# Attention and spiking feed-forward layer on one core: transfers joined to 40 a unit, the shift row sent by way of DRAM, differences loaded in four pieces, the shift's vector steps spread

## The chip, the cores and the metric

The kernel runs on one core of a Trainium2 chip, as one program. The metric is the device time of that program in microseconds (us). The engines are TensorE (PE), VectorE (DVE), ScalarE (ACT), GpSimd (POOL) and SyncE (SP); SP only issues DMA transfers here.

## The reference

One layer on x of shape (2, 2048, 256), all in float32:

```python
xn = layernorm(x)                                # per token
q, k, v = split(xn @ w_qkv)                      # 16 heads of 16
q, k = irfft(rfft(q) * sigmoid(mask)), irfft(rfft(k) * sigmoid(mask))
attn = softmax(q @ k.T / 4) @ v                  # per batch and head, 2048 x 2048 scores
a = attn @ w_out + b_out
y = square(relu(xn @ W_fc.T)) @ W_proj.T         # 256 -> 1024 -> 256
# five steps: mem = 0.9 * mem + y - (mem > 1); spikes += (mem > 1)
out = x + a + spikes / 5
```

## The kernel before

**Stages.** A first stage of about 110 us normalises x block by block, projects queries and keys (the spectral filter is folded into their weights), splits each into a high and a low part, and stores both to the DRAM tensor `qk_scratch`; values stay in SBUF. Then come 32 units, one for each head and batch (unit i = 2h + b), and a short last stage projects the attention's output and adds everything.

**A unit.** The scores of a unit are 2048 keys by 2048 queries. They are made transposed, 128 keys by 512 queries at a time, so a unit has 64 steps m (`MINI`): 4 query quarters of 16 key tiles. PE works through them in quads of 4 steps, 16 quads a unit. In each quad it does four things: scores for ACT's exponentials (`next_score`, L806); scores of a later unit's queries against keys for the row maxima (`maximum`, L773), 16 steps (`LEAD`) ahead of use; a share of the feed-forward layer (L826, L831); and, last in the quad, the four probabilities tiles of the quad before times the values (`times_v`, L821, 32 matmuls). The first quad of a quarter is an opening quad (`opening_quad`).

**Maxima and shift.** DVE reduces each maximum tile to `pmax` (L1032), one a step. When half of a unit's queries have their maxima, `split_shift` makes the shift row in four links: the negated maximum `nmax` (L1051), its high part (L1055), its low part (L1058), and a 32x32 transpose to `shiftT` (L1066). SP moves `shiftT` to `shift_rows` (`store_shift`, L361), and `first_score` (L792) adds that row to the scores through a matmul with ones. A half's row is needed at steps 0 and 32. PE's maxima go through three PSUM banks (`PLACES`), so `maximum` n+3 waits until DVE has reduced maximum n.

**Differences.** Only the first three key tiles of a quarter are computed from the keys. Every later tile accumulates on a bank that still holds the scores of the tile three before it, so it needs the key difference `delta`: POOL subtracts keys staged in `tail` (`load_stage` L335, `subtract_keys` L483), the result goes to `delta_scratch` (`store_delta`, L342), and SP loads it to `delta_sb` (`load_delta`, L351) in the pieces `PIECES`. Difference columns 0 to 127 serve step 3 of a quarter, 128 to 639 serve steps 4 to 7. Piece 0 of the next unit may be loaded only when the last quarter of this unit is done with those columns, and is needed at step 3 of the next unit.

**Who issues what.** All transfers of the units stand in SP's one queue, in the order of `head(h, b)`, and SP issues them one after the other, waiting in place:

```python
                for piece in range(len(PIECES)):
                    sp.wait_ge(exp_done, MINI * i + MINI - TB + (piece + 2) * QUAD)
                    load_delta(i + 1, piece)
```

A unit issues 76 transfers: 8 of keys, 8 of queries, 16 of staged keys, 8 that store differences, 12 that load them, 16 of shift, 8 of outputs (`move_output`, L371). POOL meanwhile squares the feed-forward's hidden values (L507) and runs the spiking steps (L522 to L541) from about step 47 on, one instruction behind the other.

## Time and profile before

| | |
|---|---|
| median of 3 runs | 1758.84 us (1754.17 to 1760.1) |
| the profiled execution, its own time | 1755.41 us |
| its span, first to last instruction | 1753.6 us |
| mean granted TensorE clock | 0.977 of 2.4 GHz |
| busy: PE, DVE, ACT, POOL | 93%, 86%, 67%, 45% of the span |
| DMA packets | 150776, 156.83 MB |

The profile is of one execution. PE is a matmul on TensorE and PEld the load of its weights, which runs beside matmuls. "A <- B" in a wait means that A stood idle until B was done. SPq is SP's queue: the time in which it issues a transfer. A row of the chain of waits names what the end of the program depended on at that time.

### The profile page before, as it was taken

Reading aid. Unit: us, or ns where it says so; the run is one execution under the profiler, and the core shown is the slowest. Engines: PE = TensorE matmul, PEld = TensorE weight load, DVE = VectorE, ACT = ScalarE, POOL = GpSimd, SP = SyncE. Lnnn points to the kernel's source line nnn. Section 1 sums busy time; section 2 is a strip of 40 time slices with the busy share of each in tenths; the row PEclk is TensorE's granted clock in tenths of the full one; section 3 lists DMA queues with packets and bytes.
Section 4 is the critical chain, followed back from the end, with each engine's and each line's share of the span. In section 5 each row is a group of like instructions: output and inputs, shape, how many; then the busy total and the mean of one; then the engine's idle time right before and its main releaser. Section 6 shows DMA issues by size and latency. Waiting matters only on the chain.

```text
span 1753.6 us, 60281 instructions
## 1 busy us (share of the span) xinstructions
PE 1634.4 (93%) x24366; PEld 1220.9 (70%) x24366; DVE 1506.6 (86%) x2782; ACT 1177.1 (67%) x2274; POOL 787.4 (45%) x1075
## 2 busy tenths in 40 slices
PE   9998999999999999999899999999999999999898
PEld 6566677677677677777676776776766776767677
DVE  7887898888898889889898898988988888889784
ACT  5546677677676677667676676776776676777572
POOL 2103345555444455555444455554344555544344
PEclk9999999999999999999999999999999999999999
DMA  6761233233222332333222323332223233322423
GB/s 225 231 224 47 69 87 82 66 87 83 80 67 71 84 80 71 83 85 82 68 74 75 84 65 84 85 84 73 68 76 85 70 78 86 83 69 73 134 58 100
DMA packets 150776, 156.83 MB, mean 89 GB/s; under 512 B 74464, under 2 KB 113248, under 8 KB 150496
## 3 DMA queue, kind: packets, MB, share of 16 engines
q1 hardware_dynamic: 147040, 149.75, 31.1%
q8 instruction: 192, 3.15, 0.7%
q10 hardware_dynamic: 3456, 3.21, 0.6%
q14 instruction: 88, 0.72, 0.1%
HBM read 119.80 MB, written 27.79 MB: 84 GB/s over the span
## 4 chain that ended last, share of the span: by engine, by line
PE 62%; DVE 16%; SPq 13%; DMA 4%; issue 3%; ACT 2%; ACTq 0%; POOL 0%; DVEq 0%; POOLq 0%
PE banks L821 22%; PE ring L773 14%; DVE pmax L1032 11%; PE ring L806 10%; PE banks L831 6%; SPq L361 4%; DMA delta_sb<-delta_scratch 4%; PE banks L826 3%; SPq L351 3%; DVE shift L1055 2%; SPq L371 2%; SPq L335 2%; ACT probs L626 2%; PE ring L942 2%; SPq L317 1%
## 5 line engine op out<-in xcount | busy, mean ns | idle before, releaser
L626 ACT ACTIVATE probs<-ring 128x512 f32<-128x512 f32 x2048 | 1076.0, 601 | 485.2 <-PE ring L806 303.7
L1032 DVE TENSOR_REDUCE pmax<-ring 128x1 f32<-128x512 f32 x2000 | 1246.5, 681 | 106.6 <-PE ring L773 98.1
L773 PE MATMUL ring<-kst,qst 64*128 64x512 f32 x2000 | 812.6, 451 | 42.3 <-DVE pmax L1032 42.3
L806 PE MATMUL ring<-qst,delta_sb 64*128 64x512 f32 x1664 | 607.9, 454 | 58.0 <-DMA delta_sb<-delta_scratch 56.4
L821 PE MATMUL banks<-probs,vst 128*32 128x128 f32 x16384 | 564.8, 279 | 0.0
L821 PEld LDWEIGHTS banks<-probs,vst 128*32 128x32 f32 x16384 | 424.1, 111 | 141.9 <-ACT probs L626 99.2
L773 PEld LDWEIGHTS ring<-kst,qst 64*128 64x128 f32 x2000 | 376.8, 188 | 180.2 <-issue 99.8
L806 PEld LDWEIGHTS ring<-qst,delta_sb 64*128 64x128 f32 x1664 | 283.1, 189 | 122.1 <-DMA delta_sb<-delta_scratch 69.8
L826 PE MATMUL banks<-xnT,wfc_sb 64*128 64x128 f32 x2016 | 279.5, 281 | 1.5 <-ACT relu_sb L631 1.5
L826 PEld LDWEIGHTS banks<-xnT,wfc_sb 64*128 64x128 f32 x2016 | 275.2, 197 | 4.9 <-ACT relu_sb L631 1.9
L831 PE MATMUL banks<-wproj_sb,hid_sb 64*128 64x256 f32 x1024 | 263.3, 377 | 0.0
L831 PEld LDWEIGHTS banks<-wproj_sb,hid_sb 64*128 64x128 f32 x1024 | 189.7, 187 | 14.2 <-ACT relu_sb L631 0.2
L792 PE MATMUL ring<-qst,kst 64*128 64x512 f32 x384 | 156.0, 470 | 10.0 <-DMA shift_rows<-shiftT 10.0
L522 POOL TENSOR_TENSOR lif<-lif 128x256 f32<-128x256 f32 x32 | 19.6, 612 | 247.3 <-ACT y_sb L646 247.3
L507 POOL TENSOR_TENSOR hid_sb<-relu_sb 128x512 f32<-128x512 f32 x64 | 66.5, 1039 | 141.7 <-ACT relu_sb L631 141.7
L794 PE MATMUL ring<-shift_rows,ones 64*128 64x512 f32 x384 | 128.0, 394 | 0.0
L483 POOL TENSOR_TENSOR tail<-tail 128x416 f32<-128x416 f32 x32 | 34.5, 1079 | 200.8 <-DMA tail<-qk_scratch 200.8
L489 POOL TENSOR_TENSOR tail<-tail 128x208 f32<-128x208 f32 x32 | 20.2, 630 | 230.8 <-ACT tail L593 230.8
L532 POOL TENSOR_SCALAR lif<-lif 128x256 f32<-128x256 f32 x128 | 109.1, 852 | 10.8
L533 POOL TENSOR_SCALAR lif<-lif 128x256 f32<-128x256 f32 x128 | 109.3, 854 | 8.0
L1100 DVE STREAM_TRANSPOSE o_sb<-banks 128x256 f32<-128x256 f32 x64 | 28.8, 450 | 93.5 <-PE banks L821 92.6
L529 POOL TENSOR_TENSOR lif<-lif 128x256 f32<-128x256 f32 x128 | 94.1, 735 | 10.0
(97 smaller groups left out, 1113.4 us busy)
## 6 DMA issues: line engine op xcount, KB each, us to landing
kst<-qk_scratch SPq DMA_DIRECT2D x256, 128.0 KB, 2.7
qst<-qk_scratch SPq DMA_DIRECT2D x256, 128.0 KB, 2.9
delta_sb<-delta_scratch SPq DMA_DIRECT2D x256, 64.0 KB, 1.9
tail<-qk_scratch SPq DMA_DIRECT2D x512, 26.0 KB, 2.2
delta_sb<-delta_scratch SPq DMA_DIRECT2D x128, 80.0 KB, 2.1
qk_scratch<-attnT SPq DMA_DIRECT2D x32, 256.0 KB, 3.0
shift_rows<-shiftT SPq DMA_DIRECT2D x512, 2.0 KB
delta_scratch<-tail SPq DMA_DIRECT2D x256, 26.0 KB, 2.0
```

Of the source, the lines that this page charges most:

```text
L529: pool.tensor_tensor(mem, upd, spks[(step + 1) % 2], ALU.subtract).then_inc(lif_step, 1)
L532: pool.tensor_scalar(spks[step % 2], mem, 1.0, None, ALU.is_gt)
L533: pool.tensor_scalar(decayed, mem, BETA, None, ALU.mult).then_inc(lif_step, 1)
L626: act.activation(probs[:, g % PS, :], score_bank(g), ACT.Exp, scale=SCALE).then_inc(exp_done, 1)
L773: pe.matmul(max_bank(x), qst[b][rows, tile * P:(tile + 1) * P], kst[b][rows, chunk * BLK:(chunk + 1) * BLK], start=True, stop=True).then_i ...
L792: pe.matmul(score_bank(g), kst[b][rows, kt * P:(kt + 1) * P], qst[b][rows, q:q + BLK], start=True, stop=False)
L794: pe.matmul(score_bank(g), ones[rows, :], shift_rows[rows, q:q + BLK], start=False, stop=True).then_inc(score_ready, 1)
L806: pe.matmul(score_bank(g), delta_sb[rows, at:at + P], qst[b][rows, q:q + BLK], start=False, stop=True, skip_group_check=True).then_inc(sco ...
L821: mm = pe.matmul(po[32 * j:32 * (j + 1), quarter * P:(quarter + 1) * P], vst[u % 2][:, kt, :], quarters[:, j], start=(kt == 0), stop=(kt = ...
L826: return pe.matmul(misc[:, (f % 4) * P:(f % 4 + 1) * P], wfc_sb[rows_of(side), c, f * P:(f + 1) * P], xnT[rows_of(side), c, tile * P:(tile ...
L831: return pe.matmul(misc[:, 0:D], hid_sb[rows_of(side), f, :], wproj_sb[rows_of(side), f, :], start=start, stop=(f == FC - 1 and side == 0))
L1032: dve.tensor_reduce(pmax[:, tile, chunk:chunk + 1], max_bank(x), AX, ALU.max).then_inc(mx_taken, 1)
```

## The change

Keys, queries, staged keys, differences and the shift row are transferred by fewer and larger DMAs, 40 a unit; the rows of a key (and of a query) lie interleaved in their 64 partitions instead of in groups of 32. The shift row goes from `shiftT` to a new DRAM tensor `shift_scratch` in one transfer and from there to `shift_rows` in two, with a wait on SP between them. The differences have a fourth piece: columns 0 to 127 alone, loaded 4 steps earlier in the last quarter and ahead of `move_output(i, 0)`; the columns from 128 on follow it. In the first half of a unit the staged keys now stand first in SP's queue, and the queries ahead of the shift. On DVE the four links stand after four successive maxima (steps 16 to 19 of a half, before all four after step 15), and the high part is made by adding a column of zeros (`shift[:, 16:24]`) instead of by a cast. On POOL `subtract_keys` stands ahead of `square`.

```diff
-PIECES = ((0, 5 * P), (5 * P, 9 * P), (9 * P, 13 * P))
+PIECES = ((0, P), (P, 5 * P), (5 * P, 9 * P), (9 * P, 13 * P))
...
 USES = 3
-KEYS = 4 * 16
+KEYS = 2 * 16
 QUERIES = 4 * 16
-SHIFT = 8 * 16
-STAGED = 16 * 16
-STORED = 8 * 16
-PIECE = 4 * 16
...
-                keys = qk_dram[1, h, :, :, tok].rearrange("d r t -> (d r) t")
-                for group in range(4):
-                    sp.dma_start(kst[b][group * 2 * DH:(group + 1) * 2 * DH, cols].bitcast(F32),
+                keys = qk_dram[1, h, :, :, tok].rearrange("d r (g t) -> (d r) g t", g=1).broadcast_to([2 * DH, 2, HALF])
+                for side in range(2):
+                    sp.dma_start(kst[b][side * SIDE:(side + 1) * SIDE, cols].bitcast(F32),
                                  keys).then_inc(keys_in[b][piece], 16)
...
                     for part in range(2):
-                        r = side * SIDE + part * 2 * DH
                         queries = qk_dram[0, h, :, part:part + 1, tok].broadcast_to([DH, 2, HALF])
-                        sp.dma_start(qst[b][r:r + 2 * DH, cols].bitcast(F32), queries).then_inc(queries_in[b][piece], 16)
+                        sp.dma_start(qst[b][side * SIDE + part:(side + 1) * SIDE:2, cols].bitcast(F32),
+                                     queries).then_inc(queries_in[b][piece], 16)
...
                 h, b = divmod(u, B)
-                for seg in range(SEGS):
-                    for k in range(2):
-                        at = b * S + k * HOP + seg * SEG
-                        sp.dma_start(stage[seg * DH:(seg + 1) * DH, k, :, :],
-                                     qk_dram[1, h, :, :, at:at + SEG]).then_inc(staged, 16)
+                for k in range(2):
+                    at = b * S + k * HOP
+                    for r in range(2):
+                        src = qk_dram[1, h, :, r, at:at + DELTA].rearrange("d (g x) -> d g x", x=SEG)
+                        sp.dma_start(stage[:, k, r, :], src).then_inc(staged, 16)
...
                 sp.wait_ge(delta_low, u + 1)
-                for seg in range(SEGS):
-                    sp.dma_start(delta_dram[u % 2, :, :, seg * SEG:(seg + 1) * SEG],
-                                 delta_pair[seg * DH:(seg + 1) * DH]).then_inc(delta_stored, 16)
+                for r in range(2):
+                    dst = delta_dram[u % 2, :, r, :].rearrange("d (g x) -> d g x", x=SEG)
+                    sp.dma_start(dst, delta_pair[:, r, :]).then_inc(delta_stored, 16)
...
-                cols = slice(*PIECES[piece])
-                src = delta_dram[u % 2, :, :, cols].rearrange("d r t -> (d r) t")
+                lo, hi = PIECES[piece]
+                src = delta_dram[u % 2, :, :, lo:hi].rearrange("d r (g t) -> (d r) g t", g=1)
                 sp.wait_ge(delta_stored, STORED * (u + 1))
-                for group in range(4):
-                    sp.dma_start(delta_sb[group * 2 * DH:(group + 1) * 2 * DH, cols].bitcast(F32),
-                                 src).then_inc(delta_in[piece], 16)
-
-            def store_shift(n, half):
+                for side in range(2):
+                    sp.dma_start(delta_sb[side * SIDE:(side + 1) * SIDE, lo:hi].bitcast(F32),
+                                 src.broadcast_to([2 * DH, 2, hi - lo])).then_inc(delta_in[piece], 16)
+
+            def store_shift(n):
                 sp.wait_ge(shift_turned, n + 1)
-                cols = slice(half * HALF, (half + 1) * HALF)
+                sp.dma_start(shift_dram[n % 2].rearrange("c (j q) -> j c q", j=4), shiftT[:, :]).then_inc(shift_stored, 16)
+
+            def load_shift(n, half):
+
+                sp.wait_ge(shift_stored, 16 * (n + 1))
+                src = shift_dram[n % 2, 0:TB, :].rearrange("(r t) x -> r (t x)", r=2)
                 for side in range(2):
-                    dst = shift_rows[side * SIDE:side * SIDE + 2, cols].rearrange("r (t j q) -> r t j q", j=4, q=32)
-                    for j in range(4):
-                        sp.dma_start(dst[:, :, j, :].bitcast(F32), shiftT[32 * j:32 * j + 16, :]).then_inc(shift_in, 16)
+                    dst = shift_rows[side * SIDE:side * SIDE + 2, half * HALF:(half + 1) * HALF]
+                    sp.dma_start(dst.bitcast(F32), src).then_inc(shift_in, 16)
...
             def head(h, b, last=False):
                 i = 2 * h + b
                 sp.wait_ge(exp_done, MINI * i + QUAD)
+                if not last:
+                    load_stage(i + 1)
                 if i and not last:
                     load_keys(h + b, 1 - b, 1)
-                if not last:
-                    load_stage(i + 1)
-                store_shift(2 * i + 1, 1)
+                    load_queries(h + b, 1 - b, 1)
+                store_shift(2 * i + 1)
+                load_shift(2 * i + 1, 1)
                 if i:
                     move_output(i - 1, 1)
-                if i and not last:
-                    load_queries(h + b, 1 - b, 1)
+                sp.wait_ge(exp_done, MINI * i + MINI // 2 + QUAD)
                 if h < H - 1:
-                    sp.wait_ge(exp_done, MINI * i + MINI // 2 + QUAD)
                     load_queries(h + 1, b, 0)
                 if last:
                     sp.wait_ge(misc_full, use(i - 1, UP_B) + 1)
                     store_delta(i + 1)
-                    store_shift(2 * i + 2, 0)
+                    store_shift(2 * i + 2)
+                    load_shift(2 * i + 2, 0)
                 if h < H - 1:
                     sp.wait_ge(exp_done, MINI * i + MINI - TB + QUAD)
                     load_keys(h + 1, b, 0)
-                move_output(i, 0)
-                if not last:
-                    for piece in range(len(PIECES)):
-                        sp.wait_ge(exp_done, MINI * i + MINI - TB + (piece + 2) * QUAD)
-                        load_delta(i + 1, piece)
+                for piece in range(0 if last else len(PIECES)):
+                    sp.wait_ge(exp_done, MINI * i + MINI - TB + (piece + 1) * QUAD)
+                    load_delta(i + 1, piece)
+                    if piece == 0:
+                        move_output(i, 0)
+                if last:
+                    move_output(i, 0)
             for i in range(2 * (H - 1)):
                 head(i // 2, i % 2)
...
                     stage_v(h + b, 1 - b, MINI * i + PS)
+                if not last:
+                    subtract_keys(i + 1)
                 square(i, 1, UP_B)
                 if not last:
-                    subtract_keys(i + 1)
                     low_delta(i + 1)
                 n = LIF_LINKS * i
...
                                       negate=True).then_inc(max_step, 1)
                 if link == 1:
                     dve.wait_ge(max_step, 2 * n + 1)
-                    dve.tensor_copy(shift[:, 0:8].bitcast(F32R), nmax[:]).then_inc(max_step, 1)
+                    if n == 0:
+                        dve.wait_ge(shift_blank, 1)
+                    dve.tensor_tensor(shift[:, 0:8].bitcast(F32R), nmax[:], shift[:, 16:24], ALU.add).then_inc(max_step, 1)
                 if link == 2:
...
                     scale_output(2 * i - 1)
-                if m == LEAD - 1:
-                    for link in range(4):
-                        split_shift(link, 2 * i + 1, 1, CHUNKS * (i + 1))
+                if 0 <= m - LEAD < 4:
+                    split_shift(m - LEAD, 2 * i + 1, 1, CHUNKS * (i + 1))
```

Two places in the order of the instructions, each as the program issues them. The first is **DVE** around the shift row that is made in the second half of a unit; the names are those of the section on the kernel. Before:

```order
L1032 TENSOR_REDUCE pmax<-ring 128x1 [waits mx_ready] x4
L1051 TENSOR_REDUCE nmax<-pmax 128x8 [waits mx_taken]
L1055 CAST shift<-nmax 128x8 [waits max_step]
L1058 TENSOR_TENSOR shift<-nmax,shift 128x8 [waits max_step]
L1066 STREAM_TRANSPOSE shiftT<-shift 128x32 [waits shift_in,shift_split]
L1032 TENSOR_REDUCE pmax<-ring 128x1 [waits mx_ready] x8
L1120 STREAM_TRANSPOSE o_turned<-o_scaled 128x256 [waits out_moved1_0,normalised]
```

After the change:

```order
L1043 TENSOR_REDUCE pmax<-ring 128x1 [waits mx_ready] x5
L1062 TENSOR_REDUCE nmax<-pmax 128x8 [waits mx_taken]
L1043 TENSOR_REDUCE pmax<-ring 128x1 [waits mx_ready]
L1068 TENSOR_TENSOR shift<-nmax,shift 128x8 [waits max_step]
L1043 TENSOR_REDUCE pmax<-ring 128x1 [waits mx_ready]
L1071 TENSOR_TENSOR shift<-nmax,shift 128x8 [waits max_step]
L1043 TENSOR_REDUCE pmax<-ring 128x1 [waits mx_ready]
L1077 STREAM_TRANSPOSE shiftT<-shift 128x32 [waits shift_in,shift_split]
L1043 TENSOR_REDUCE pmax<-ring 128x1 [waits mx_ready] x4
L1131 STREAM_TRANSPOSE o_turned<-o_scaled 128x256 [waits out_moved1_0,normalised]
```

The links no longer follow each other: one maximum stands between any two of them, and the transpose comes four maxima later. The second place is **SP** at the end of a unit, from the stored differences to the first loads of the next unit's differences. Before:

```order
L342 DMA delta_scratch<-tail 32x1x208 [waits delta_low]
L342 DMA delta_scratch<-tail 32x1x208 x7
L361 DMA shift_rows<-shiftT 2x8x32 [waits shift_turned]
L361 DMA shift_rows<-shiftT 2x8x32 x7
L317 DMA kst<-qk_scratch 32x1024 [waits exp_done]
L317 DMA kst<-qk_scratch 32x1024 x3
L371 DMA attnT<-o_turned 16x8x32 [waits out_turned]
L371 DMA attnT<-o_turned 16x8x32 x3
L351 DMA delta_sb<-delta_scratch 32x640 [waits delta_stored,exp_done]
L351 DMA delta_sb<-delta_scratch 32x640 x3
```

After the change:

```order
L345 DMA delta_scratch<-tail 16x8x208 [waits delta_low]
L345 DMA delta_scratch<-tail 16x8x208
L359 DMA shift_scratch<-shiftT 4x32x32 [waits shift_turned]
L367 DMA shift_rows<-shift_scratch 2x1024 [waits shift_stored]
L367 DMA shift_rows<-shift_scratch 2x1024
L319 DMA kst<-qk_scratch 64x1x1024 [waits exp_done]
L319 DMA kst<-qk_scratch 64x1x1024
L353 DMA delta_sb<-delta_scratch 64x1x128 [waits delta_stored,exp_done]
L353 DMA delta_sb<-delta_scratch 64x1x128
L377 DMA attnT<-o_turned 16x8x32 [waits out_turned]
L377 DMA attnT<-o_turned 16x8x32 x3
L353 DMA delta_sb<-delta_scratch 64x1x512 [waits delta_stored,exp_done]
L353 DMA delta_sb<-delta_scratch 64x1x512
```

Between `shift_turned` and the first load of differences there were 16 issues and there are now 5, with a wait for `shift_stored` among them; the four issues of outputs stand now between the first and the second piece.

## Rows read from the trace of the kernel before

**Rows 1.** The page: busy time of an engine; engines' shares of the chain that ended last.

```profile
PE 1634.4 (93%) x24366; PEld 1220.9 (70%) x24366; DVE 1506.6 (86%) x2782; ACT 1177.1 (67%) x2274; POOL 787.4 (45%) x1075
...
PE 62%; DVE 16%; SPq 13%; DMA 4%; issue 3%; ACT 2%; ACTq 0%; POOL 0%; DVEq 0%; POOLq 0%
```

**Rows 2.** Who waited for whom: us in total, times, longest wait in us.

```profile
PEld ring L806 <- DMA delta_sb<-delta_scratch: 69.8, 31, 3.4
PEld ring L773 <- DVE pmax L1032: 62.1, 69, 1.4
...
PEld ring L792 <- DMA shift_rows<-shiftT: 12.0, 7, 5.8
```

**Rows 3.** The chain in order of time, 376 to 430 us: start us, us, what.

```profile
376.85 1.18 PE banks L821 x32
...
380.88 1.06 PE banks L821 x32
...
390.66 1.01 PE banks L821 x32
...
398.82 1.01 PE banks L821 x32
...
401.82 1.01 PE banks L821 x32
...
404.54 1.01 PE banks L821 x32
...
408.73 2.50 DVE pmax L1032 x4
...
424.92 2.09 DMA delta_sb<-delta_scratch
...
427.56 1.01 PE banks L821 x32
```

**Rows 4.** The chain over the whole span: the same wait 29 units apart.

```profile
174.59 2.02 DMA delta_sb<-delta_scratch
...
1623.34 2.05 DMA delta_sb<-delta_scratch
```

**Rows 5.** PE, PEld, DVE, ACT, POOL busy in a stretch; PEclk, DMA share, GB/s.

```profile
376.50:380.50 4.00, 4.00 (x49) 3.17 (x49) 2.00 (x4) 1.69 (x4) 3.70 (x5) 0.63 0.40 105
```

**Rows 6.** Timeline of PE, 409 to 415 us: start us, us, engine, line, operation.

```profile
409.90 1.08 PE L821 MATMUL banks<-probs,vst 128*32 128x128 f32 x32
...
413.56 1.08 PE L821 MATMUL banks<-probs,vst 128*32 128x128 f32 x32
```

**Rows 7.** Timeline of DVE, 392 to 428 us.

```profile
411.47 0.35 DVE L1055 CAST shift<-nmax 128x8 fp32r<-128x8 f32 x1
411.86 0.17 DVE L1058 TENSOR_TENSOR shift<-nmax,shift 128x8 fp32r<-128x8 f32 x1
```

**Rows 8.** Timeline of POOL, 398 to 432 us.

```profile
411.18 0.61 POOL L522 TENSOR_TENSOR lif<-lif 128x256 f32<-128x256 f32 x1 [7.27 <-ACT y_sb L646]
```

**Rows 9.** One line's instructions (DVE): ns min/median/max, first and last start.

```profile
L1055 DVE CAST shift<-nmax x64: 172/487/997, 98.1 to 1689.9; 128x8 fp32r<-128x8 f32 x64
...
L1109 DVE TENSOR_TENSOR o_scaled<-o_sb,rden x64: 281/282/785, 157.6 to 1723.7; 128x128 f32<-128x128 f32 x64
```

**Rows 10.** Timeline of SP's queue, 376 to 430 us; a row joins its issues.

```profile
381.52 10.82 SPq L335 DMA_DIRECT2D tail<-qk_scratch  x16
...
412.30 5.31 SPq L361 DMA_DIRECT2D shift_rows<-shiftT  x8
417.65 1.79 SPq L317 DMA_DIRECT2D kst<-qk_scratch  x4
```

**Rows 11.** The chain, 139 to 156 us: the old shift transfer's landing.

```profile
144.48 1.65 DMA shift_rows<-shiftT
```

**Rows 12.** DMA issues of the page: count, KB each, median us to landing.

```profile
delta_scratch<-tail SPq DMA_DIRECT2D x256, 26.0 KB, 2.0
...
attnT<-o_turned SPq DMA_DIRECT2D x256, 16.0 KB, 1.9
```

More of the change, by code:

```diff
@@ L58 @@
 USES = 3
-KEYS = 4 * 16
+KEYS = 2 * 16
 QUERIES = 4 * 16
-SHIFT = 8 * 16
-STAGED = 16 * 16
-STORED = 8 * 16
-PIECE = 4 * 16
+SHIFT = 2 * 16
+STAGED = 4 * 16
+STORED = 2 * 16
+PIECE = 2 * 16
 RUNS = 5
@@ L235, in build @@
         shift_turned = sem("shift_turned")
+        shift_stored = sem("shift_stored")
         shift_in = sem("shift_in")
@@ L1155, in beside_maxima @@
                     scale_output(2 * i)
-                if m == MINI // 2 + LEAD - 1 and not last:
-                    for link in range(4):
-                        split_shift(link, 2 * i + 2, 0, CHUNKS * (i + 1) + CHUNKS // 2)
+                if 0 <= m - LEAD - MINI // 2 < 4 and not last:
+                    split_shift(m - LEAD - MINI // 2, 2 * i + 2, 0, CHUNKS * (i + 1) + CHUNKS // 2)
                 if m == MINI // 2 + LEAD + 7:
```

6 lines of the change are left out of this document (3 added, 3 removed).

## The prediction

> **What bounds the kernel now.** I began with the page. PE is busy 93% of the span and DVE 86%, but the chain that ended last is PE for only 62%; DVE has 16% of it and SP's queue 13% [rows 1]. An issuing engine with 13% of the chain is what to look for. The waits name three: PE stood for the load of differences 31 times, 69.8 us; for DVE's maxima 62.1 us; for the shift row 12.0 us, of which one wait alone is 5.8 [rows 2].
>
> To price a unit I read the gaps between the passes that close each quad (L821) in the chain. An undisturbed gap is 404.54 - 401.82 = 2.72 us, and one that holds an opening quad 401.82 - 398.82 = 3.00 [rows 3]. So PE alone needs 12 x 2.72 + 4 x 3.00 = 44.6 us a unit. A unit takes (1623.34 - 174.59) / 29 = 49.96 us [rows 4]. The 5.3 us between them lie in three places:
>
> - after step 15 of a unit: 390.66 - 380.88 = 9.78 for two plain gaps and one opening gap (8.44), a loss of 1.34 [rows 3]
> - after step 47: 413.56 - 409.90 = 3.66 where 3.00 would do, a loss of 0.66 [rows 6]
> - around the start of a unit: the rest, 3.32, with the wait for differences (69.8 / 31 = 2.25) in it [rows 2]. The other 1.07 is largely the clock. After the wait in rows 3 the next gap is 4.03 instead of 2.72, and the granted clock of that stretch is 0.63 [rows 5], thus partly its lower level of 1.2 GHz; PE had been idle just before.
>
> The wait for differences is SP's doing. From the moment `shiftT` is made (412.30) SP issues 8 shift transfers, 4 of keys, 4 outputs and then 4 of differences, the last at 424.92, which lands at 427.01 [rows 3, 10]. Nothing in this row of issues waits for an engine; it is issue time.
>
> **The change, part by part.**
>
> *Issue time.* Two-dimensional transfers cost 1.79 / 4 = 0.45 us of SP each, those of three dimensions 5.31 / 8 = 0.66 and 10.82 / 16 = 0.68 [rows 10]. Joined transfers have three dimensions, as the shapes in the order show, so I take 0.66 for each, and 0.46 for the two loads of the shift row. Forty of them are some 26 us where 76 now take about 46 of the unit's 50.
>
> *The end of a unit, anew.* Let T be the end of the transpose to `shiftT`. The old T is 412.28 [rows 10]. Now four more maxima stand before it, at a busy DVE's pace of 2.50 / 4 = 0.625 [rows 3], and the cheaper high part saves 0.19: T = 412.28 + 2.50 - 0.19 = 414.6. From T on SP does the following: the store of the shift and the wait for its landing, L; two loads of the row, 0.92; keys, 1.32; piece 0, 1.32; outputs, 4 x 0.66 = 2.64; one issue of piece 1, 0.66; the second issue and landing of piece 1, 2.1 as in rows 3.
>
> L is in no row. A store of differences to DRAM lands 2.0 us after its issue [rows 12]. The outputs have the shift's 16 KB in the same runs of 32 numbers and land in 1.9, the old shift transfer with an eighth of them in 1.65 [rows 11, 12]; so more runs cost some 0.25. I take L = 2.2. The low bound is 1.65. For the high one, the new store's first dimension is 4 where that of the outputs is 16: if the rows of the first dimension are what works in parallel, the part of 1.9 beyond an issue (1.3) counts fourfold, L = 0.6 + 5.2 = 5.8. I stay at the low end because the old transfer, whose first dimension is 2, is no slower than the others.
>
> Piece 0 then lands at T + 2.2 + 0.92 + 1.32 + 0.66 + 2.1 = T + 7.2. It is needed at step 3, in the opening quad that starts at about T + 7.8 (below), behind the scores of steps 0 to 2: hidden. Piece 1 lands at T + 11.2. It is needed when the second quad of the next unit starts. The quad after step 51 starts without its 0.66 of loss at 413.56 + 1.01 - 0.66 = 413.9; three plain quads, an opening one and 0.34 of DVE's delay (below) later it is 425.4, T + 10.8. So a stall of about 0.4 to 0.5 us stays and moves one quad on: SP, not the data, is late, now with the four outputs in front. A stall that short should leave the clock up. Loss at the start of a unit: 3.32 before, 0.5 after; gain 2.8.
>
> The shift row itself lands at T + 2.2 + 0.92 + 1.6 = T + 4.7 and is needed three quads after 413.9, at T + 7.8: hidden with 3 us to spare. If this cover goes, each us shows in PE at both halves.
>
> *DVE's links.* Four maxima take 2.5 us of a 2.72 us quad, 3.00 if it opens. Four links at once push the next maximum past PE's three banks. Spread, the maximum of step 48 is reduced first and PE goes on. Laid out by hand, DVE ends step 51 with its links 3.8 us after the opening quad began, and PE's fourth maximum of the next quad waits 0.14; the turn of the outputs, which now follows a quad later instead of two, adds 0.2. Loss 0.34 a half.
>
> The cast goes. It takes 0.17 at least and 1.00 at most [rows 9]: at 411.47 it ends with POOL's instruction of 411.18 to 411.79 [rows 8], 0.35. The add that takes its place has a row of its form, L1058, 0.17 [rows 7]. Is it free of POOL? L1109, also two inputs in SBUF, has a median of 0.28 and a maximum of 0.785 [rows 9], so such an instruction can be held by up to 0.5. In the first half POOL has just finished its square, in the second it runs without a pause. I take 0.34 for the first half and, with two adds held for 0.2 each on average, 0.75 for the second (bounds 0.34 and 1.3). Sum 1.1, where 2.0 were lost; gain 0.9.
>
> The Trainium skill's page SBUF — State Buffer, section Who interferes with whom, says that a DVE instruction with two SBUF inputs contends with a GpSimd instruction that reads SBUF, by a full block. L1109 agrees with it; the 64 runs of L1058 with the 0.17 seen here do not show it. By that rule the add would be no better than the cast while POOL is busy.
>
> *The rest.* Staged keys land earlier; POOL's subtraction then stands ahead of the square and finds its data, and POOL has slack (45% busy) [rows 1]. The wait of 5.8 us in unit 0 stands behind 16 issues of staged keys, which become 4; a like one is in unit 30, behind 6 loads of x. Both go: 12 us, and some 2 us of lower clock after them.
>
> **Sum.** Gain a unit 2.8 + 0.9 = 3.7, less 0.1 for L1109 meeting POOL more often: 3.6. Over units 1 to 30 that is 108 us. Unit 0 and unit 30 give 14 more, the first start and unit 0's links about 2. In all 124: the profiled execution's 1755.4 becomes 1631. The median of the runs stands 3 us above this execution, so I say 1633.
>
> **Rivals.**
>
> - *The stall moves to piece 1 at nearly full size.* For it: SP waits in place for L, and four outputs stand ahead. With L = 3.7 the stall is 2 us, and gaps of 4.03 after it return in part (0.5). Against the forecast 2.0 a unit: 60 us, 1693.
> - *Nothing is left at the start, and no add is held.* L = 1.65 and issues a little cheaper: 0.9 a unit less, 1606.
> - *DVE becomes the bound.* Its maxima alone are 64 x 0.625 = 40 us of a unit of 46.3, and it is busy 86% now, 43 us of 49.96 [rows 1]. Against: 3 us spare by that. For: its work is uneven, and POOL may hold it 1 us more. 1661 with that us in each unit.
> - *SP's issue time was not the limit*, the joined transfers cost in issue and landing what the small ones did: 1750. Against: 0.66 a transfer whatever its size [rows 10].
> - *Slower: the shift's store is slow.* From L = 5.2 on both halves wait for the row, and piece 1 is 3 us late with the clock down after it. The loss is (L - 2.2) + 2 x (L - 5.2) + about 1.3 of clock against 3.6 of gain, so it decides from about L = 4.9; with L = 5.8 a unit loses 2.5: 1755 + 75 - 14 = 1815.
>
> The Trainium skill's page DMA: Bandwidth & Descriptors, section Why a DMA increments its semaphore by 16 and not by 1, says that a transfer uses the largest number of engines, up to 16, that divides the slowest dimension of both sides. By it the new store has 4 engines and 32 runs on each, the outputs 16 and 8, and this last rival is its upper end.
>
> **Chances.** Forecast (1605 to 1660) 0.62; stall moved 0.17; nothing left, below 1605, 0.09; DVE the bound above 1660 0.05; no limit of SP 0.03; slow store 0.04. The range that leaves out no more than 2 in 10 is 1602 to 1695. A measurement of this kernel tells some 0.3% from no change. Faster by more 0.94, within it 0.02, slower 0.04.
>
> **What would show it.** Right: PE's wait on `delta_sb` falls from 2.25 to about 0.5 a unit, on the piece of columns 128 on; no wait on `shift_rows`; clock near 1.0; four closing gaps of 3.3 to 3.8 in place of 4.3 and 3.7; SP idle before `shift_turned`. Wrong: a landing of `shift_scratch` over 3.5 us, issues of joined transfers over 0.8, the add at L1068 at 0.5 or more, or an idle PE that waits for DVE after step 3.

## The result, and the profile after

The changed kernel takes 1619.35 us (median of 4 runs, 1616.07 to 1624.41), the one before, on the same chip, 1756.51 (4 runs, 1753.72 to 1760.1). The ratio is 0.9221, with a 95% interval of 0.9189 to 0.9252: 137 us less, where 124 were forecast. The experiments below were timed in three groups, each with the kernel before beside them; its medians there were 1754.26 to 1755.28, and each ratio is to that of the same group.

The page of the changed kernel, for comparison with [rows 1] and the DMA rows of [rows 12]:

```profile
span 1617.7 us, 59194 instructions
...
PE 1584.3 (98%) x24366; PEld 1197.1 (74%) x24366; DVE 1467.7 (91%) x2782; ACT 1172.8 (72%) x2274; POOL 787.5 (49%) x1075
...
PE 85%; DMA 5%; SPq 5%; ACT 2%; issue 1%; DVE 1%; ACTq 0%; POOL 0%; POOLq 0%
...
kst<-qk_scratch SPq DMA_DIRECT2D x128, 256.0 KB, 4.0
...
delta_sb<-delta_scratch SPq DMA_DIRECT2D x192, 128.0 KB, 2.7
...
delta_scratch<-tail SPq DMA_DIRECT2D x64, 104.0 KB, 2.3
```

PE now has 85% of the chain instead of 62%. DVE went from 16% to 1%, SP's queue from 13% to 5%. The mean granted clock is 0.998.

Its waits, beside [rows 2]:

```profile
DVE pmax L1043 <- PE ring L784: 91.6, 284, 3.4
...
PEld ring L817 <- DMA delta_sb<-delta_scratch: 30.7, 29, 3.2
```

PE's wait for DVE's maxima, 62.1 us before, is 3.5 us in 14 waits. DVE waits for PE as before, 91.6 us where it was 98.1. The wait for differences is 30.7 instead of 69.8 us, 1.06 a unit. The chain where it falls, beside [rows 3]:

```profile
426.87 1.01 PE banks L832 x32
...
429.58 1.01 PE banks L832 x32
...
436.30 0.55 SPq L353
436.89 2.84 DMA delta_sb<-delta_scratch
...
441.45 1.01 PE banks L832 x32
...
444.16 1.01 PE banks L832 x32
```

The plain gap behind the stall is 444.16 - 441.45 = 2.71, and the granted clock from 437 to 446 us is 1.00. Before, such a gap was 4.03, at 0.63: the clock no longer falls there. SP's queue, beside [rows 10]:

```profile
428.20 0.54 SPq L359 DMA_DIRECT2D shift_scratch<-shiftT  x1
430.15 0.53 SPq L367 DMA_DIRECT2D shift_rows<-shift_scratch  x2
430.72 1.20 SPq L319 DMA_DIRECT2D kst<-qk_scratch  x2
432.02 1.18 SPq L353 DMA_DIRECT2D delta_sb<-delta_scratch  x2
433.25 2.95 SPq L377 DMA_DIRECT2D attnT<-o_turned  x4
436.30 3.76 SPq L353 DMA_DIRECT2D delta_sb<-delta_scratch  x6
```

This is the critical stretch in six rows. From the store of the shift to SP's next issue, 430.15 - 428.20 = 1.95 us pass; over 62 such places the median is 1.98, one took 5.63. Then keys, piece 0 and the four outputs stand ahead of piece 1, which is issued from 436.30 on. (In the diff of the section on the change, the stores of the differences and of the second half's shift stand under `if not last:`, so every unit but the last has them.)

The starts of the 2048 exponentials, 64 a unit, give every kernel's loss by place, in its profiled execution. Given here are means over units 2 to 29, quads counted from 0. Without any loss a plain quad takes 2.72 by these starts, an opening one 2.80 and the one ahead of it 2.92, together as much as the 2.72 and 3.00 of the closing gaps. "Start" is the first two quads, "links" quads 4, 5, 6 and 12, where the shift's links fall. The last two columns are the lengths of units 0 and 30. All in us:

| kernel | median time | a unit | start | links | unit 0 | unit 30 |
|---|---|---|---|---|---|---|
| before | 1756.51 | 49.89 | 3.20 | 1.93 | 58.9 | 56.7 |
| after | 1619.35 | 46.08 | 1.26 | 0.17 | 46.2 | 47.4 |
| before_order | 1806.46 | 51.62 | 4.61 | 1.96 | 60.5 | 58.1 |
| before_dve | 1796.07 | 51.21 | 6.51 | 0.03 | 59.7 | 58.2 |
| scratch_only | 1668.28 | 47.29 | 0.68 | 1.97 | 52.4 | 53.8 |
| joined_only | 1696.49 | 48.74 | 2.09 | 1.89 | 48.3 | 46.8 |
| shift_direct | 1766.79 | 50.73 | 5.95 | 0.03 | 47.4 | 51.2 |
| links_together | 1639.67 | 46.71 | 0.02 | 2.06 | 47.2 | 46.5 |
| three_pieces | 1630.72 | 46.38 | 1.60 | 0.05 | 46.6 | 45.5 |
| cast_spread | 1622.41 | 46.21 | 1.42 | 0.12 | 46.6 | 47.2 |
| keys_behind | 1595.22 | 45.06 | 0.08 | 0.34 | 46.1 | 50.5 |
| out_behind | 1597.26 | 45.14 | 0.15 | 0.37 | 46.5 | 50.8 |
| best | 1590.18 | 45.01 | 0.12 | 0.28 | 47.2 | 44.9 |
| best2 | 1584.09 | 44.85 | 0.18 | 0.05 | 47.2 | 44.7 |

"Before" in this table is the run beside the changed kernel.

### The profile page after: what moved, and what is told of

Same layout as the page of the kernel before. It is cut to its first block, busy times and chain, and to the rows that moved or that the text cites. A ratio compares the mean times of both kernels' runs of the same rounds, so it can differ in the third digit from the quotient of the medians.

```text
span 1617.7 us, 59194 instructions
## 1 busy us (share of the span) xinstructions
PE 1584.3 (98%) x24366; PEld 1197.1 (74%) x24366; DVE 1467.7 (91%) x2782; ACT 1172.8 (72%) x2274; POOL 787.5 (49%) x1075
## 4 chain that ended last, share of the span: by engine, by line
PE 85%; DMA 5%; SPq 5%; ACT 2%; issue 1%; DVE 1%; ACTq 0%; POOL 0%; POOLq 0%
PE banks L832 28%; PE ring L784 18%; PE ring L817 14%; PE banks L842 9%; PE banks L837 6%; DMA delta_sb<-delta_scratch 5%; SPq L377 3%; PE ring L803 2%; PE banks L721 2%; PE ring L953 2%; SPq L353 2%; PE ring L805 1%; ACT probs L637 1%; PE ring L734 1%; PE ring L707 1%
## 5 line engine op out<-in xcount | busy, mean ns | idle before, releaser
L1043 DVE TENSOR_REDUCE pmax<-ring 128x1 f32<-128x512 f32 x2000 | 1262.8, 682 | 98.6 <-PE ring L784 91.6
L784 PE MATMUL ring<-kst,qst 64*128 64x512 f32 x2000 | 795.2, 446 | 0.2 <-DMA kst<-qk_scratch 0.2
L817 PE MATMUL ring<-qst,delta_sb 64*128 64x512 f32 x1664 | 586.4, 444 | 23.3 <-DMA delta_sb<-delta_scratch 21.6
L832 PE MATMUL banks<-probs,vst 128*32 128x128 f32 x16384 | 554.4, 276 | 0.0
L784 PEld LDWEIGHTS ring<-kst,qst 64*128 64x128 f32 x2000 | 367.4, 184 | 123.4 <-issue 97.2
L817 PEld LDWEIGHTS ring<-qst,delta_sb 64*128 64x128 f32 x1664 | 272.3, 184 | 81.1 <-ACT probs L637 46.1
L837 PE MATMUL banks<-xnT,wfc_sb 64*128 64x128 f32 x2016 | 266.3, 272 | 1.5 <-ACT relu_sb L642 1.5
L837 PEld LDWEIGHTS banks<-xnT,wfc_sb 64*128 64x128 f32 x2016 | 261.5, 188 | 4.6 <-ACT relu_sb L642 1.9
L533 POOL TENSOR_TENSOR lif<-lif 128x256 f32<-128x256 f32 x32 | 20.1, 627 | 245.9 <-ACT y_sb L657 245.9
L540 POOL TENSOR_TENSOR lif<-lif 128x256 f32<-128x256 f32 x128 | 94.6, 739 | 10.0
L542 POOL TENSOR_TENSOR lif<-lif 128x256 f32<-128x256 f32 x128 | 94.6, 739 | 10.0
L538 POOL TENSOR_TENSOR lif<-lif,y_sb 128x256 f32<-128x256 f32 x128 | 94.2, 736 | 8.1
L517 POOL TENSOR_TENSOR hid_sb<-relu_sb 128x512 f32<-128x512 f32 x64 | 66.4, 1038 | 20.5 <-ACT relu_sb L642 20.5
```

The source lines that it names most:

```text
L540: pool.tensor_tensor(mem, upd, spks[(step + 1) % 2], ALU.subtract).then_inc(lif_step, 1)
L784: pe.matmul(max_bank(x), qst[b][rows, tile * P:(tile + 1) * P], kst[b][rows, chunk * BLK:(chunk + 1) * BLK], start=True, stop=True).then_i ...
L817: pe.matmul(score_bank(g), delta_sb[rows, at:at + P], qst[b][rows, q:q + BLK], start=False, stop=True, skip_group_check=True).then_inc(sco ...
L832: mm = pe.matmul(po[32 * j:32 * (j + 1), quarter * P:(quarter + 1) * P], vst[u % 2][:, kt, :], quarters[:, j], start=(kt == 0), stop=(kt = ...
L837: return pe.matmul(misc[:, (f % 4) * P:(f % 4 + 1) * P], wfc_sb[rows_of(side), c, f * P:(f + 1) * P], xnT[rows_of(side), c, tile * P:(tile ...
L1043: dve.tensor_reduce(pmax[:, tile, chunk:chunk + 1], max_bank(x), AX, ALU.max).then_inc(mx_taken, 1)
```

## Experiments

Theory A is the prediction's: SP's in-order queue between the shift and the differences sets the start of a unit, and DVE's links the rest. Theory B says that the number of issues did it, so that joining alone would bring the gain. Theory C says that the four pieces in their new order did it.

### Parts of the change on the kernel before

**before_order**: the kernel before, with the differences in four pieces and in the new order, nothing else.

```diff
-PIECES = ((0, 5 * P), (5 * P, 9 * P), (9 * P, 13 * P))
+PIECES = ((0, P), (P, 5 * P), (5 * P, 9 * P), (9 * P, 13 * P))
...
-                move_output(i, 0)
-                if not last:
-                    for piece in range(len(PIECES)):
-                        sp.wait_ge(exp_done, MINI * i + MINI - TB + (piece + 2) * QUAD)
-                        load_delta(i + 1, piece)
+                for piece in range(0 if last else len(PIECES)):
+                    sp.wait_ge(exp_done, MINI * i + MINI - TB + (piece + 1) * QUAD)
+                    load_delta(i + 1, piece)
+                    if piece == 0:
+                        move_output(i, 0)
+                if last:
+                    move_output(i, 0)
```

> The kernel before with one part of the change alone: four pieces of differences, loaded a quad earlier, the outputs between the first and the second piece. No transfer is joined, the links stay together. Theory A (issue time is what makes the differences late, the order only moves it): from the transpose SP issues 8 shift transfers, 4 keys, 4 of the first piece, 4 outputs, 4 of the second, which lands about 15 us after it where PE needs it after 13. The first wait goes, a second of 2 us comes: 1735 to 1757. Rival B (the early first piece was the gain): the wait halves as in the changed kernel, 1690 to 1710.

Measured: 1806.46 us, ratio 1.0296 (1.0275 to 1.0318). PE's wait for differences is now

```profile
PEld ring L808 <- DMA delta_sb<-delta_scratch: 94.3, 35, 4.1
```

instead of 69.8, at a clock of 0.964. As a cause of the gain, theory C falls: alone, the new order costs 50 us. Theory A had the place right and the time wrong. The wait did move to the second piece: in the unit around 430 us its last issue stands behind the outputs and lands at 438.86, 16.4 us after SP began with the shift. But 15 us and no loss (1735 to 1757) were expected. The four issues more add to a queue that is already late, and the quad behind that wait runs in part at a granted clock of 0.50 (1.2 GHz).

**before_dve**: the kernel before, with the links spread and the add in place of the cast.

```diff
-                if m == LEAD - 1:
-                    for link in range(4):
-                        split_shift(link, 2 * i + 1, 1, CHUNKS * (i + 1))
+                if 0 <= m - LEAD < 4:
+                    split_shift(m - LEAD, 2 * i + 1, 1, CHUNKS * (i + 1))
```

(likewise in the second half)

> The kernel before with DVE's part of the change alone: links spread over four maxima, the add for the cast. Theory A: the closing gaps around the links fall from 4.3 and 3.7 to 3.0 to 3.1, 2 us a unit, but the shift row is made 2.3 us later and SP, whose queue is full, passes this on to the differences: the wait at the start grows by 2 to 2.3 us. Net 1745 to 1775. Rival B (the parts add up): 2 us a unit less, 1690 to 1700.

Measured: 1796.07 us, ratio 1.0241 (1.0219 to 1.0264), 21 us above theory A's range. The links lose 0.03 a unit instead of 1.93, and the start loses 6.51 instead of 3.20:

```profile
PEld ring L806 <- DMA delta_sb<-delta_scratch: 142.3, 32, 5.5
```

SP's queue in this kernel:

```profile
421.05 5.29 SPq L361 DMA_DIRECT2D shift_rows<-shiftT  x8
426.39 2.37 SPq L317 DMA_DIRECT2D kst<-qk_scratch  x4
428.80 2.59 SPq L371 DMA_DIRECT2D attnT<-o_turned  x4
431.50 5.62 SPq L351 DMA_DIRECT2D delta_sb<-delta_scratch  x12
```

Spreading makes `shiftT` some two us late, everything behind it in the queue is late by that, and PE pays it in full, 3.3 us at a mean clock of 0.948 (0.977 before). The last link was not free: it is the head of SP's chain.

**scratch_only**: the kernel before, with the shift row sent by way of DRAM, nothing else.

```diff
-                for side in range(2):
-                    dst = shift_rows[side * SIDE:side * SIDE + 2, cols].rearrange("r (t j q) -> r t j q", j=4, q=32)
-                    for j in range(4):
-                        sp.dma_start(dst[:, :, j, :].bitcast(F32), shiftT[32 * j:32 * j + 16, :]).then_inc(shift_in, 16)
+                sp.dma_start(shift_dram[n % 2].rearrange("c (j q) -> j c q", j=4), shiftT[:, :]).then_inc(shift_stored, 16)
...
+                for side in range(2):
+                    dst = shift_rows[side * SIDE:side * SIDE + 2, half * HALF:(half + 1) * HALF]
+                    sp.dma_start(dst.bitcast(F32), src).then_inc(shift_in, 16)
```

> The other part alone: the kernel before with only the shift row sent by way of DRAM (one transfer, a wait, two transfers in place of eight). Theory A: SP's way from the transpose is 2.5 us instead of 5.3, all behind it comes 2.8 us earlier, the wait of 2.25 us a unit goes, both link losses stay; the waits of units 0 and 30 stay in part, since sixteen staged transfers stand ahead: 1655 to 1685. Rival B (SP's whole queue is the limit, 41 of 50 us are still issues, so it is late elsewhere): 1700 or more.

Measured: 1668.28 us, ratio 0.9503 (0.9483 to 0.9522), inside theory A's range. The queue of this kernel, in the first half of a unit:

```profile
419.32 0.58 SPq L359 DMA_DIRECT2D shift_scratch<-shiftT  x1
421.32 0.53 SPq L367 DMA_DIRECT2D shift_rows<-shift_scratch  x2
421.89 3.06 SPq L377 DMA_DIRECT2D attnT<-o_turned  x4
```

SP is done with the shift after 421.89 - 419.32 = 2.6 us, its stand for the landing included, where eight issues took 5.31 [rows 10]; the median of both halves is 2.5. That cuts the start loss from 3.20 to 0.68. Of the parts tried alone it is worth the most: 88 us.

**joined_only**: keys, staged keys and differences joined, with the new order of a unit's first half (three pieces behind the outputs, as before); the shift still in eight transfers, links together, cast kept.

```diff
-PIECES = ((0, P), (P, 5 * P), (5 * P, 9 * P), (9 * P, 13 * P))
+PIECES = ((0, 5 * P), (5 * P, 9 * P), (9 * P, 13 * P))
...
-SHIFT = 2 * 16
+SHIFT = 8 * 16
```

(against after; the unit's last loads, the links and the shift transfers are as before; the new order of SP's first half, and POOL's subtraction ahead of the square, stay in)

> One part of the change alone: keys, staged keys and differences in joined transfers (and the first half's new order). Three pieces behind the outputs, the links together with the cast, and the shift in eight transfers are as before the change. Theory A: from the transpose to the landing of the first piece SP now needs 5.3 + 1.3 + 2.6 + 0.7 + 2.8 = 12.7 us where it needed 14.7; the wait of 2.25 us a unit nearly goes and the clock stays up, while both link losses stay. Also the two waits of units 0 and 30 go: 1650 to 1675. Rival B (landing grows with size and takes it back): 1700 or more.

Measured: 1696.49 us, ratio 0.9659 (0.9635 to 0.9684), between the two theories. The wait for differences is

```profile
PEld ring L815 <- DMA delta_sb<-delta_scratch: 47.7, 30, 2.5
```

From the first shift transfer to the last issue of piece 0 there are 16 issues instead of 20, but a joined piece lands in 2.8 to 3.0 us by the page, not in 1.9 to 2.1. Units 0 and 30 fall to 48.3 and 46.8 from 58.9 and 56.7: 20 us there, by joining together with the new order of the first half.

### Parts taken out of the changed kernel

**shift_direct**: after, with the shift in eight transfers again and no DRAM tensor.

```diff
-                sp.dma_start(shift_dram[n % 2].rearrange("c (j q) -> j c q", j=4), shiftT[:, :]).then_inc(shift_stored, 16)
...
-                    dst = shift_rows[side * SIDE:side * SIDE + 2, half * HALF:(half + 1) * HALF]
-                    sp.dma_start(dst.bitcast(F32), src).then_inc(shift_in, 16)
+                    dst = shift_rows[side * SIDE:side * SIDE + 2, cols].rearrange("r (t j q) -> r t j q", j=4, q=32)
+                    for j in range(4):
+                        sp.dma_start(dst[:, :, j, :].bitcast(F32), shiftT[32 * j:32 * j + 16, :]).then_inc(shift_in, 16)
```

> The changed kernel with the shift row moved from SBUF to SBUF in eight transfers again, without the DRAM tensor. Theory A: SP needs 5.3 us for them where the way by DRAM takes 2.5 with its wait, so keys and both first pieces are 2.7 us later; the start of a unit loses 2.7 us more and the clock falls after some of the waits: 1700 to 1730. Rival B (the shift's way is beside the chain, the four outputs are what counts): within 15 us of 1619.

Measured: 1766.79 us, ratio 1.0075 (1.0048 to 1.0102). Without this one part the whole gain is gone. PE waits twice a unit, for piece 0 and again for piece 1, and a stretch over both (columns as in [rows 5]) has the clock at 0.72:

```profile
PEld ring L817 <- DMA delta_sb<-delta_scratch: 112.9, 61, 3.2
```

```profile
416.00:428.00 12.00, 9.75 (x116) 7.21 (x117) 6.40 (x12) 5.28 (x11) 10.80 (x16) 0.72 0.56 157
```

Theory A expected 2.7 us more at the start of a unit; it is 4.7 more (5.95 instead of 1.26), and the time is 37 us over its range. The mean clock is 0.948 where it was 0.998, which is at most 88 us of PE's time, an estimate (0.05 x 1763). The granted clock falls behind the two waits, to 0.58 from 420.6 to 428 us, so in part to 1.2 GHz.

**three_pieces**: after, with three pieces behind the outputs, as before.

```diff
-PIECES = ((0, P), (P, 5 * P), (5 * P, 9 * P), (9 * P, 13 * P))
+PIECES = ((0, 5 * P), (5 * P, 9 * P), (9 * P, 13 * P))
...
-                for piece in range(0 if last else len(PIECES)):
-                    sp.wait_ge(exp_done, MINI * i + MINI - TB + (piece + 1) * QUAD)
-                    load_delta(i + 1, piece)
-                    if piece == 0:
-                        move_output(i, 0)
+                move_output(i, 0)
+                if not last:
+                    for piece in range(len(PIECES)):
+                        sp.wait_ge(exp_done, MINI * i + MINI - TB + (piece + 2) * QUAD)
+                        load_delta(i + 1, piece)
```

> The changed kernel with three pieces (columns 0 to 639 first), loaded behind the outputs and 4 steps later, as before the change; all transfers stay joined. Theory A (both the joining and the early first piece shorten the start): the first piece lands where the second does now, but is needed 1.5 us earlier, in the opening quad; the wait grows from 1.06 to about 2.5 us a unit, and the clock falls again after some: 1660 to 1690. Rival B (joining did it all): within 10 us of 1619. Rival C (the split did it all): back near 1700 or above, 3.3 us a unit.

Measured: 1630.72 us, ratio 0.93 (0.9271 to 0.933). The fourth piece and its order bring 11 us, where theory A had 41 to 71: the start loses 1.60, not some 2.5. They make room for piece 0 and leave the outputs ahead of piece 1, so the stall only changes its place.

**links_together**: after, with the four links in a row again, the add kept (the diff of before_dve backwards, in both halves).

> The changed kernel with the four links of the shift in a row again after step 15 of each half, the add kept. Theory A: spreading is worth more than dropping the cast. The closing gaps around the links, 3.0 to 3.1 now, grow to about 3.5 (second half) and 3.9 (first half, where POOL's square holds the add), 1.3 us a unit; but the shift row is ready 2.3 us earlier, so the wait for the second piece (1.06 us a unit) goes. Net 1612 to 1632, with both moves to be seen in the gaps. Rival B: the add alone made the links cheap; then the gaps stay at 3.1 and the time falls to about 1590.

Measured: 1639.67 us, ratio 0.9341 (0.9321 to 0.9361). The start loss vanishes (0.02), since `shiftT` comes earlier, and the links' loss returns in full, 2.06:

```profile
PEld ring L784 <- DVE pmax L1043: 62.9, 63, 1.5
...
PEld ring L817 <- DMA delta_sb<-delta_scratch: 0.6, 1, 0.6
```

I had expected 1.3 for the links, and the time is 8 us above the range. Spreading is thus a trade: 1.9 us of DVE against 1.2 of SP.

**cast_spread**: after, with the cast in place of the add.

```diff
-                    dve.tensor_tensor(shift[:, 0:8].bitcast(F32R), nmax[:], shift[:, 16:24], ALU.add).then_inc(max_step, 1)
+                    dve.tensor_copy(shift[:, 0:8].bitcast(F32R), nmax[:]).then_inc(max_step, 1)
```

> The changed kernel with the cast in place of the add, links still spread. Theory A (the cast was costly only because the links followed each other and POOL held it): spread, its extra 0.2 to 0.8 us falls into DVE's idle time, 0.24 us a quad, and little of it shows: 1619 to 1630. Rival B (each us in which POOL holds DVE shows in full): 0.2 us in one half and 0.4 more in the other, 31 units: 1638 or more.

Measured: 1622.41 us, ratio 0.9242 (0.9221 to 0.9263), inside theory A's range; the interval overlaps that of after. The add is worth nothing that can be measured.

### What is left, taken away

**out_behind**: after, with the outputs behind piece 1.

```diff
-                    if piece == 0:
+                    if piece == 1:
                         move_output(i, 0)
```

> The changed kernel with one edit: the four outputs stand behind the second piece of differences in SP's queue, not ahead of it. Theory A: what is left of the stall at a unit's start (PE's weight loads wait 30.7 us in 29 units for the second piece) is issue time of SP, 3.0 to 3.4 us of it the four outputs. The second piece then lands some 3 us earlier, the wait is gone and a unit takes 44.8 to 45.0 instead of 46.1 us: 1583 to 1592 us. Rival B: the landing itself is late (2.8 us now, 2.0 before, with twice the bytes in each transfer and the keys' transfers just ahead of it); then the wait shrinks by less than half and the time stays above 1605.

Measured: 1597.26 us, ratio 0.9099 (0.9079 to 0.9119). The wait goes, as theory A has it:

```profile
PEld ring L817 <- DMA delta_sb<-delta_scratch: 2.2, 5, 0.8
```

Its 5 us above the expected range are largely in unit 30, 50.8 us, where the shift stands behind six loads of x.

**keys_behind**: after, with the keys behind the last piece, a different transfer out of the way.

```diff
-                if h < H - 1:
-                    sp.wait_ge(exp_done, MINI * i + MINI - TB + QUAD)
-                    load_keys(h + 1, b, 0)
...
+                if h < H - 1:
+                    load_keys(h + 1, b, 0)
```

> The changed kernel with the two key transfers behind the last piece of differences, the outputs still between the first and the second. Theory A (the second piece is late by SP's issues in front of it): it is issued 1.2 us earlier, its landing stays at 2.8 us, and the wait of 1.06 us a unit falls below 0.2: 1592 to 1600. Theory B (half a megabyte of keys in flight makes the landing longer): the same, and the landing falls from 2.8 to 2.4 us or less. Rival C: neither, 1610 or more.

Measured: 1595.22 us, ratio 0.9086 (0.9068 to 0.9105), as theory A has it. Theory B falls: the landing of piece 1 has a median of 2.8 us here and in after. A start loss of 0.08: it makes no difference which transfer leaves, only that SP comes to piece 1 earlier. Its page tells something about landings:

```profile
delta_sb<-delta_scratch SPq DMA_DIRECT2D x192, 128.0 KB, 2.8
...
delta_sb<-delta_scratch SPq DMA_DIRECT2D x64, 32.0 KB, 2.1
```

In after, with 512 KB of keys just ahead, the same 32 KB piece lands in 3.2; the 128 KB ones are unchanged.

**best**: out_behind, with the first half's links three steps later, past POOL's square, and the loads of x spread over six units.

```diff
-                if 0 <= m - LEAD < 4:
-                    split_shift(m - LEAD, 2 * i + 1, 1, CHUNKS * (i + 1))
+                if 0 <= m - LEAD - 3 < 4:
+                    split_shift(m - LEAD - 3, 2 * i + 1, 1, CHUNKS * (i + 1))
```

> The version with the outputs behind the second piece, and two more edits: the first half's links stand at steps 19 to 22 (POOL's square, which holds the add for up to 0.8 us, is over by then), and the six loads of x stand one each behind six units instead of together ahead of unit 30. Theory A: the gap of 3.06 after step 19 becomes 2.72 (10 us in all) and unit 30 loses its 5 us: 1580 to 1587. Rival B: the add meets another instruction of POOL, or the shift row is late for step 32 since it is made 2 us later: 1597 or more.

Measured: 1590.18 us, ratio 0.9063 (0.9044 to 0.9082), 3 us over the range. Unit 30 fell from 50.8 to 44.9. The gap in quad 5 went (3.06 to 2.72), but one of 2.96 came in quad 6, where the turn of the outputs now adjoins the links.

**best2**: best, with that turn four steps later.

```diff
-                if m == LEAD + 7 and i:
+                if m == LEAD + 11 and i:
```

> The best version so far (1590.2 us) with one edit: the first half's turn of the outputs stands at step 27, four steps after the transpose of the shift, not right behind it. Theory A: the gap of 2.96 us that this quad has now becomes 2.72; 0.24 us in 31 units, 7 us: 1581 to 1585. Rival B (the gap has another cause, or the turn costs the same a quad later): 1590.

Measured: 1584.09 us, ratio 0.9024 (0.9005 to 0.9042), as expected: 35 us below the changed kernel. A unit takes 44.85 us against a floor of 44.64, so PE is nearly all that bounds it: PE has 96% of the chain. From 410 to 446 us, over the start of a unit, the chain has PE's lines alone:

```profile
423.30 1.01 PE banks L834 x32
...
426.02 1.01 PE banks L834 x32
...
428.74 1.01 PE banks L834 x32
...
431.76 1.01 PE banks L834 x32
```

## Why the prediction was right, step by step

**The mechanism.** Right. The start of a unit hung on SP's issues from `shiftT` on. Alone, scratch_only shortens just this path and takes 2.5 of the 3.2 us away; before_dve makes `shiftT` later and the loss doubles; out_behind and keys_behind take 3 and 1.2 us of issues out of the path and the loss is gone. The 40 issues of the unit from 394.85 us on take 25.8 us of SP, where 26 were forecast.

**"A stall of about 0.4 to 0.5 us stays and moves one quad on."** It moved to piece 1, as forecast. The stall's size was too small: the start loss has a median of 1.00 and a mean of 1.26, where 0.5 stood. Of the terms, T falls at 428.17 and piece 1 lands at 436.89 + 2.84 = 439.73, T + 11.6 instead of T + 11.2. Two terms were too small: the landing of a joined piece, taken as 2.1 from an 80 KB load and measured at 2.84 with 128 KB, and the four outputs, 3.05 instead of 2.64. The rest was 0.75 too large, L (1.98 instead of 2.2) and the two loads of the row (0.57 instead of 0.92) above all; that the sum is off by 0.4 only is in part luck. Two units of the 28 lose 4.7 each; in them the landing takes 4.4 to 4.5 us and the clock falls, in no other unit. The chain's rows of these landings:

```profile
342.74 4.48 DMA delta_sb<-delta_scratch
...
1171.31 4.41 DMA delta_sb<-delta_scratch
```

The stretch over the first of them, at a mean granted clock of 0.85, so in part at 1.2 GHz:

```profile
340.00:350.00 10.00, 7.15 (x99) 5.62 (x93) 6.16 (x10) 5.00 (x10) 8.88 (x13) 0.85 0.42 119
```

Why these two landed late no run here shows.

**"A stall that short should leave the clock up."** Right for 26 of 28 units. The mean clock is 0.998, and 0.7 us of stall in the chain above is followed by a plain gap of 2.71.

**Links: "Sum 1.1, where 2.0 were lost."** Mis-sized: 0.17 is lost, so the gain is 1.8 a unit instead of 0.9. Timeline of DVE in the changed kernel, second half of a unit:

```profile
426.02 0.68 DVE L1043 TENSOR_REDUCE pmax<-ring 128x1 f32<-128x512 f32 x1
426.62 0.16 DVE L1068 TENSOR_TENSOR shift<-nmax,shift 128x8 fp32r<-128x8 f32 x1
426.69 0.69 DVE L1043 TENSOR_REDUCE pmax<-ring 128x1 f32<-128x512 f32 x1
427.29 0.16 DVE L1071 TENSOR_TENSOR shift<-nmax,shift 128x8 fp32r<-128x8 f32 x1
427.37 0.69 DVE L1043 TENSOR_REDUCE pmax<-ring 128x1 f32<-128x512 f32 x1
427.97 0.20 DVE L1077 STREAM_TRANSPOSE shiftT<-shift 128x32 f32<-128x32 f32 x1
```

From one maximum's start to the next are 0.67 and 0.68 us with a link between them, where 0.625 is the pace without one. A link that stands between two independent maxima overlaps them and costs some 0.05 us. In a row each waits for the one before: in links_together these two start 0.20 us apart, and one that POOL holds costs more, 0.39 in [rows 7].

```profile
383.27 0.17 DVE L1071 TENSOR_TENSOR shift<-nmax,shift 128x8 fp32r<-128x8 f32 x1
383.47 0.21 DVE L1077 STREAM_TRANSPOSE shiftT<-shift 128x32 f32<-128x32 f32 x1
```

I had costed the links at their full durations.

**"With two adds held for 0.2 each on average" in the second half.** Wrong in place. None is held there: L1068 takes 0.156 to 0.159 us in all 31 second halves. The first half's takes 0.46 on average, so it is held by 0.3, and 14 of 32 take 0.5 or more. I had named that as a sign of being wrong; it was none. It costs what quad 5 loses, 0.14 us a unit (0.34 in out_behind), and the cast, which is held likewise, costs no more. One of them:

```profile
404.25 0.50 DVE L1068 TENSOR_TENSOR shift<-nmax,shift 128x8 fp32r<-128x8 f32 x1
```

POOL's instructions beside the two:

```profile
403.68 1.03 POOL L517 TENSOR_TENSOR hid_sb<-relu_sb 128x512 f32<-128x512 f32 x1
...
425.74 0.86 POOL L534 TENSOR_SCALAR lif<-y_sb 128x256 f32<-128x256 f32 x1
426.65 0.85 POOL L535 TENSOR_SCALAR lif<-y_sb 128x256 f32<-128x256 f32 x1
```

The add at 404.25 lies within the square and is held. In the second half L1068 at 426.62 starts between L534 and L535 and runs into L535, and L1071 at 427.29 lies within L535; neither is held, and so it is in 31 of 31 units. In links_together, where L1068 falls into L533 instead, a TENSOR_TENSOR, it takes 0.35 in 31 of 31. So it is the place that decides. The Trainium skill's page SBUF — State Buffer, section Who interferes with whom, has a DVE instruction with two SBUF inputs contend with a GpSimd instruction that reads SBUF. This trace agrees for POOL's TENSOR_TENSOR and not for its TENSOR_SCALAR. Whether the operation decides or the number of its SBUF inputs (L517 and L533 have two, L535 one) no run here shows.

**Units 0 and 30.** 14 us were forecast beside 3.6 each; measured are 12.7 and 9.3 in all, 22 against 21.2. In joined_only 20 of them are there already, from joining or from the new order of the first half; the two were not tried apart.

**The sum.** Start 1.9 (forecast 2.8) and links 1.8 (forecast 0.9) make 3.7 a unit; the unit as a whole is 3.8 shorter, where 3.6 were forecast. Two terms were off by 0.9, in opposite directions, and that they cancelled is luck: the middle of the forecast was better than its parts. The 0.1 set aside for L1109 did not show. (In the rivals, 1 us in each of 30 units on top of 1633 is 1663, not 1661.)

**The rivals.** A slow store of the shift is refuted: L has a median of 1.98 us, with a first dimension of 4. The Trainium skill's page DMA: Bandwidth & Descriptors, section Why a DMA increments its semaphore by 16 and not by 1, gives such a transfer 4 engines; whether it had four no row tells, but it cost nothing here. DVE as the bound is refuted: in the units PE waits 3.5 us in all for its maxima, and DVE has 1% of the chain. That SP's issues were no limit is refuted by scratch_only. The stall at full size (2 us) did not come, since L was short, but over half of it did.

**What stays open.** The parts alone give -88 (scratch), -60 (joined), +50 (order), and +40 (links and add), together -58; all at once give -137. The runs show why they don't add up: spreading and the fourth piece cost only while SP is late, and each of the first two alone leaves SP late. How much of the losses of before_order, before_dve and shift_direct is the clock and how much the stall was not separated. An upper bound by the mean granted clock times the span, an estimate: 23 us more than in before for before_order, 52 for before_dve, and the 88 above for shift_direct. The new order of the first half and POOL's subtraction ahead of the square were never taken away alone.

## What to carry to other kernels

Price a queue from the event that starts it to the deadline, issue by issue, and order it by deadlines: here one transfer group behind what PE needs next was worth 22 us, in a line of code. Spreading dependent small instructions between large independent ones hides them almost wholly but makes their product later, so look first who waits for the product; where nobody has slack, it costs more than it brings. When transfers are joined, take the landing from a row of the new size.

## What the runs showed of the hardware

- SP issues a transfer of two rows in about 0.27 us (0.53 for two), less than a two-dimensional one of 32 partitions (0.45) and one of three dimensions (medians of 0.58 to 0.61 in the changed kernel; single ones took up to 1.8).
- Landings grow with the size and with what is queued ahead: differences 1.9 to 2.1 us at 64 to 80 KB, 2.7 to 2.8 at 128 KB; 32 KB lands in 3.2 behind 512 KB of keys and in 2.1 without (keys_behind).
- A store of 16 KB to DRAM whose first dimension is 4 is seen as landed by SP 1.98 us after its issue (median), about as fast as the 16 KB transfers of the outputs (2.0), whose first dimension is 16.
- A DVE instruction with two SBUF inputs of 128x8 is held by POOL's TENSOR_TENSOR (0.50 instead of 0.16 us, up to 0.99) and not by its TENSOR_SCALAR (31 of 31).
- Such a small instruction between two independent maxima (TENSOR_REDUCE, 128x512 from PSUM) adds some 0.05 us from start to start, in a row with others that it depends on 0.20.
